# Convolution taps as diagonal matmuls, sums copied out by the scalar engine, gate product on GpSimd, front steps reordered

## The reference

```python
h   = concat(patch_embed(x), text_embed(...))       # (64, 48, 192)
x1  = layernorm(h)
# bidirectional Mamba, inner width 384, 16 states, 4 taps; dir 1 runs over the reversed sequence
xz  = x1 @ in_w.T;  xc, z = split(xz)
xconv = conv_b + sum(conv_w[:, k] * xpad[:, k:k + L, :] for k in range(K))   # K = 4
u   = silu(xconv)
dtx, Bm, Cm = split(u @ xproj_w.T)
dt  = softplus(dtx @ dt_w.T + dt_b)
h_t = exp(dt * A) * h_{t-1} + dt * Bm * u            # 16 states a channel
y   = sum_n(h_t * Cm) + u * D
y   = y * silu(z)                                    # the gate
out = y @ out_w.T
# layernorm, residual, then a mixture of 8 experts (top 2), expert width 768
```

## Time and profile before

| | us |
|---|---|
| three runs, median (lowest, highest) | 2037.2 (2034.75, 2037.57) |
| the profiled execution, its own time | 2037.6 |
| its span, first to last instruction | 2035.9 |
| TensorE matmul busy | 1523.3 (75%) |
| VectorE busy | 1514.1 (74%) |
| GpSimd busy | 1056.5 (52%) |
| ScalarE busy | 861.1 (42%) |

### The profile page before, as it was taken

How to read it: one execution, slowest core, us unless ns; L and a number is a source line. 1 busy time by engine, 2 the same in 40 slices (tenths; PEclk the granted TensorE clock), 3 DMA queues, 4 the chain that set the end, 5 groups by cost and what they waited for, 6 DMA issues and landing times. The chain is left out here.

```text
span 2035.9 us, 19521 instructions
## 1 busy us (share of the span) xinstructions
PE 1523.3 (75%) x4714; PEld 866.1 (43%) x4715; DVE 1514.1 (74%) x1780; ACT 861.1 (42%) x1848; POOL 1056.5 (52%) x539
## 2 busy tenths in 40 slices
PE   6566776776677677767767775876643899999997
PEld 4233343343344334434433443443332566666665
DVE  3699999999999999999999999999954122222221
ACT  2555545554554555455455454554510222222221
POOL 2465676675667657655675675548600233333332
PEclk8777897888788778878878887888875999999999
DMA  3412303031231303122130402213025411111111
GB/s 80 148 48 79 119 29 136 21 129 52 85 114 35 136 16 133 38 99 97 53 120 18 147 37 100 85 42 136 0 73 133 114 26 24 25 24 24 26 24 22
DMA packets 49182, 144.71 MB, mean 71 GB/s; under 512 B 13118, under 2 KB 26028, under 8 KB 48332
## 3 DMA queue, kind: packets, MB, share of 16 engines
q1 hardware_dynamic: 36956, 129.61, 18.7%
q0 software_dynamic: 12144, 14.30, 4.2%
HBM read 132.67 MB, written 11.21 MB: 71 GB/s over the span
## 5 line engine op out<-in xcount | busy, mean ns | idle before, releaser
L629 POOL TENSOR_TENSOR ring<-dtu,brep 128x1536 f32<-128x1536 f32 x192 | 661.0, 3447 | 446.0 <-DVE states L640 316.3
L652 PE MATMUL py<-ring,ident 128*128 128x384 f32 x1536 | 637.2, 568 | 133.7 <-DVE yg L669 110.5
L640 DVE TENSOR_TENSOR_SCAN states<-states,ring 128x768 f32<-128x768 f32 x384 | 673.7, 1755 | 30.2 <-ACT states L616 14.7
L652 PEld LDWEIGHTS py<-ring,ident 128*128 128x128 f32 x1536 | 332.7, 223 | 420.6 <-issue 186.2
L616 ACT ACTIVATE states<-dt_,aneg 128x376 f32<-128x376 f32 x768 | 406.1, 560 | 0.0
L642 DVE TENSOR_TENSOR ring<-states,crep 128x768 f32<-128x768 f32 x384 | 367.6, 957 | 13.2
L613 ACT ACTIVATE states<-zero_cols 128x16 f32<-128x16 f32 x384 | 71.2, 186 | 642.7 <-DVE ring L642 637.6
L1288 PE MATMUL gu<-w,xsT 96*128 x660 | 298.3, 602 | 7.2 <-issue 6.6
L462 PE MATMUL pf<-xT,wxz 97*128 97x384 f32 (+1 forms) x384 | 183.7, 624 | 139.0 <-ACT xT L449 55.3
L1329 DVE COPY yidx<-place 128x1 int32 (+1 forms) x56 | 8.4, 153 | 250.8 <-DMA out_tokens<-ys,yidx 250.8
L1288 PEld LDWEIGHTS gu<-w,xsT 96*128 96x128 f32 x660 | 122.6, 193 | 145.6 <-issue 145.6
(11 more groups left out here) (221 smaller groups left out, 1412.3 us busy)
## 6 DMA issues: line engine op xcount, KB each, us to landing
brep<-b_c_rows SPq DMA_DIRECT2D x64, 768.0 KB, 4.1
crep<-b_c_rows SPq DMA_DIRECT2D x64, 768.0 KB, 4.6
w<-in_w SPq DMA_DIRECT2D x8, 1152.0 KB, 14.2
wd<-in_wd SPq DMA_DIRECT2D x8, 576.0 KB, 16.3
ptok<-in_p_tok SPq DMA_DIRECT2D x8, 384.0 KB, 3.8
pT<-in_p_T SPq DMA_DIRECT2D x8, 384.0 KB, 4.8
out_tokens<-h SPq DMA_DIRECT2D x8, 288.0 KB, 2.1
x_scratch<-x SPq DMA_DIRECT2D x8, 288.0 KB, 2.9
```

The costliest lines, as they stand in the source:

```text
L629: gp.tensor_tensor(ring[:, w % NRING], dtu[:, d, o, :].unsqueeze(1).to_broadcast([128, GN, T]), brep[:, ng], ALU.mult).then_inc(dbu_ok, 1)
L640: v.tensor_tensor_scan(h_in, h_in, x_in, 0.0, ALU.mult, ALU.add).then_inc(scan_ok, 1)
L652: mm = pe.matmul(py[:, 0:T], ident[:], ring[:, w % NRING, i, :], start=(ng == 0 and i == 0), stop=False)
```

## The change

Four edits, one after the other:

1. The convolution leaves VectorE. At setup VectorE builds 12 diagonal matrices (3 tiles x 4 taps) from the identity. `pe_conv` adds all four taps of a tile in PSUM with them; the moving operand is a shifted window of `xc`. ScalarE no longer writes the scaled copy. The bias is added when a tile is read: tile 0 by a copy to `ea` in its own step, tiles 1 and 2 in the SiLU itself. The SiLU is three instructions of one tile instead of one of three, and it comes ahead of the SiLU of z, which has its own semaphore.
2. The sums leave `py` by ScalarE (`act_y`), unit `TAKEN` = 4 after the tile's start, at the end of a unit's main work; the next tile's first sum waits for this copy (`y_sb`).
3. The gate product is done by GpSimd in place in `yg` (`pool_gate`), one unit later, behind that unit's ring fill.
4. One table `DIR` replaces `DIR0` and `DIR1`. A front matmul stands one unit after the copy that it waits for or that frees its bank; the step times are made as tiles 0 and 1, then 2, instead of 0, then 1 and 2. Most steps of `BACK` are one unit later; `xT_out` is one earlier.

```diff
+        tap_diag = sb("tap_diag", [128, NC, KC + 1, 128])
...
+            conv = [(f"cv{d}_{o}", 1) for o in range(NC)]
             rest = [(f"bc{d}", 1)] + [(f"dt{d}_{o}", 1) for o in range(NC)]
-            FJOBS += x + rest + z if d == 0 else x + z[:2] + rest + z[2:]
+            FJOBS += x + conv + rest + z
...
-            if tiles[0] == 0:
-                wait(act, dv.sem, dv.after("dt", e - 1))
...
-                    act.activation(out, p[:, 0:T].rearrange("p (b l) -> p b l", b=CB), ACT.Copy)
-
-                    op = act.activation(ea[:, o, :], p[:, 0:T], ACT.Identity, scale=cw[:, o, KC:KC + 1], bias=cb[:, o:o + 1])
+                    op = act.activation(out, p[:, 0:T].rearrange("p (b l) -> p b l", b=CB), ACT.Copy)
...
+        def pe_conv(pe, c, d, tiles):
+
+            for o in tiles:
+                job_read(pe, f"xz{d}_{o}", c)
+                p = job_start(pe, f"cv{d}_{o}", c)
+                for k in range(KC + 1):
+                    at = k if d == 0 else 2 * KC - k
+                    mm = pe.matmul(p[:, 0:T], tap_diag[:, o, k, :], xc[:, o, :, at:at + L], start=(k == 0), stop=(k == KC))
+                mm.then_inc(jsem(f"cv{d}_{o}", "full"), 1)
+
+        def act_conv(act, c, d):
 
             e = 2 * c + d
...
+            p = job_wait(act, f"cv{d}_0", c)
+            wait(act, dv.sem, dv.after("dt", e - 1))
+            act.activation(ea[:, 0, :], p[:, 0:T], ACT.Identity, bias=cb[:, 0:1]).then_inc(jsem(f"cv{d}_0", "free"), 1)
 
         def act_silu(act, c, d):
 
             e = 2 * c + d
             act.preload_act_table_set("silu_and_others")
+            if not isinstance(c, int) or c < NCH:
+                job_read(act, f"cv{d}_0", c)
+                wait(act, y_ok, UD * (e - 1))
+                act.activation(u[:, d, 0], ea[:, 0], ACT.Silu).then_inc(ds.sem, 1)
+                for o in range(1, NC):
+                    p = job_wait(act, f"cv{d}_{o}", c)
+                    act.activation(u[:, d, o], p[:, 0:T], ACT.Silu, bias=cb[:, o:o + 1]).then_inc(jsem(f"cv{d}_{o}", "free"), 1)
             if not isinstance(e, int) or e > 0:
...
-                op = act.activation(zs[:, 1 - d], zs[:, 1 - d], ACT.Silu)
...
-                op = act.activation(u[:, d], ea[:], ACT.Silu)
-            op.then_inc(ds.sem, 1)
+                act.activation(zs[:, 1 - d], zs[:, 1 - d], ACT.Silu).then_inc(zs_ok, 1)
             act.preload_act_table_set("natural_log_exp_and_others")
...
             if ng == 0:
-                wait(pe, gated, NC * e + o)
+                wait(pe, y_sb, NC * e + o)
...
+        def act_y(act, c, d, o):
+
+            wait(act, qfull, QJ * (c - 1) + 2)
+            act.wait_ge(filled, 32)
+            act.wait_ge(y_ok, U2 * c + UD * d + NG * (o + 1))
+            for lo, hi in ((0, LI), (LI, L)):
+                yv = py[:, 0:T].rearrange("p (b l) -> p b l", b=CB)[:, :, lo:hi]
+                op = act.activation(yg[:, d, o, CB * lo:CB * hi].rearrange("p (b l) -> p b l", b=CB), yv, ACT.Copy)
+            op.then_inc(y_sb, 1)
+
+        def pool_gate(gp, c, d, o):
 
             e = 2 * c + d
...
+            gp.wait_ge(zs_ok, e + 1)
+            gp.wait_ge(y_sb, NC * e + o + 1)
             for lo, hi in ((0, LI), (LI, L)):
...
+                op = gp.tensor_tensor(yv, yv, zv, ALU.mult)
             op.then_inc(gated, 1)
...
+                for k in range(KC + 1):
+                    v.tensor_scalar(tap_diag[:, o, k, :], ident[:], cw[:, o, k:k + 1], None, ALU.mult)
...
-                 7: ["embed", "embed_rs"], 8: ["x1"], 9: ["xT"], 10: ["xT_out"]}
-        DIR0 = {-2: ["x01"], -1: ["x01_out", "x2"], 0: ["x2_out", "conv01"], 1: ["conv2", "silu", "bc"],
-                2: ["bc_out"], 3: ["bc_store"], 4: ["dt0"], 5: ["dt12", "dt0_out"], 7: ["dt12_out", "softplus"],
-                8: ["z01"], 9: ["steps", "z01_out", "z2"], 10: ["z2_out"]}
-        DIR1 = {-2: ["x01"], -1: ["x01_out", "x2"], 0: ["x2_out", "conv01"],
-                1: ["z01", "conv2", "silu", "z01_out"], 2: ["bc", "bc_out"], 3: ["bc_store"], 5: ["dt0"],
-                7: ["dt0_out", "dt12"], 8: ["dt12_out", "softplus", "z2"], 9: ["z2_out", "steps"]}
-        BACK = {2: ["out01"], 3: ["out01_add", "out2"], 4: ["out2_add"], 5: ["rs"], 6: ["h2"],
-                8: ["stat3", "rs3"], 9: ["x3"], 15: ["x3T0"], 17: ["x3T0_out", "x3T1"], 19: ["x3T1_out"],
-                20: ["router"], 23: ["logits"]}
+                 7: ["embed", "embed_rs"], 8: ["x1"], 9: ["xT", "xT_out"]}
+        DIR = {-2: ["x01"], -1: ["x01_out"], 0: ["x2", "conv0", "x2_out", "conv0_out"], 1: ["conv12", "silu"],
+               3: ["bc", "bc_out"], 4: ["bc_store", "dt01", "dt01_out"], 5: ["dt2"], 6: ["dt2_out", "softplus"],
+               7: ["z01", "z01_out"], 8: ["steps", "z2", "z2_out"]}
+        BACK = {3: ["out01"], 4: ["out01_add", "out2"], 5: ["out2_add"], 6: ["rs"], 7: ["h2"],
+                9: ["stat3", "rs3"], 10: ["x3"], 16: ["x3T0"], 18: ["x3T0_out", "x3T1"], 20: ["x3T1_out"],
+                21: ["router"], 23: ["logits"]}
...
-        GATE = NG + 1
+        TAKEN = NG
...
+            for step, at in (("y_out", TAKEN), ("gate", TAKEN + 1)):
...
-                yield from gates[w]
                 yield "scan", c, w
...
+                yield from taken[w]
                 yield from slots[w]
```

More of the change, by code:

```diff
@@ L505, in act_silu @@
                 job_read(act, f"xz{before[1]}_{2 * NC - 2}", before[0])
-                op = act.activation(zs[:, 1 - d], zs[:, 1 - d], ACT.Silu)
-            if not isinstance(c, int) or c < NCH:
-                act.wait_ge(dv.sem, dv.after("conv2b", e))
-                wait(act, y_ok, UD * (e - 1))
-                op = act.activation(u[:, d], ea[:], ACT.Silu)
-            op.then_inc(ds.sem, 1)
+                act.activation(zs[:, 1 - d], zs[:, 1 - d], ACT.Silu).then_inc(zs_ok, 1)
             act.preload_act_table_set("natural_log_exp_and_others")
@@ L516, in pe_bc @@
             pe.wait_ge(ds.sem, ds.after("silu", e))
+            for o in range(1, NC):
+                job_read(pe, f"cv{d}_{o}", c)
             p = job_start(pe, f"bc{d}", c)
@@ L656, in pe_sum @@
             mm.then_inc(y_ok, 1)
[L658 removed]
+        def act_y(act, c, d, o):
[7 more added lines that the diff above has]
+        def pool_gate(gp, c, d, o):
             e = 2 * c + d
[L662 to L665 removed]
+            gp.wait_ge(zs_ok, e + 1)
+            gp.wait_ge(y_sb, NC * e + o + 1)
             for lo, hi in ((0, LI), (LI, L)):
[L667 to L669 removed]
+                zv = zs[:, d, o, :].rearrange("p (b l) -> p b l", b=CB)[:, :, lo:hi]
+                yv = yg[:, d, o, CB * lo:CB * hi].rearrange("p (b l) -> p b l", b=CB)
+                op = gp.tensor_tensor(yv, yv, zv, ALU.mult)
             op.then_inc(gated, 1)
@@ L943, in plan @@
                             spread[w + U2].append(("spread", c + 1, (d, ng, which)))
-            gates = [[] for _ in range(U2)]
-            for d in range(2):
-                for o in range(NC):
-                    w = UD * d + NG * o + GATE
-                    if w < U2:
-                        gates[w].append(("gate", c, (d, o)))
-                    elif not first:
-                        gates[w - U2].append(("gate", c - 1, (d, o)))
-            put(DIR1, 0, c, 1)
+            taken = [[] for _ in range(U2)]
+            for step, at in (("y_out", TAKEN), ("gate", TAKEN + 1)):
+                for d in range(2):
+                    for o in range(NC):
+                        w = UD * d + NG * o + at
+                        if w < U2:
+                            taken[w].append((step, c, (d, o)))
+                        elif not first:
+                            taken[w - U2].append((step, c - 1, (d, o)))
+            put(DIR, 0, c, 1)
             if not first:
@@ L994, in prologue @@
             gates = ("z01", "z01_out", "z2", "z2_out")
-            direction = list(in_order(DIR0, 0, 0))
+            direction = list(in_order(DIR, 0, 0))
             yield from [step for step in direction if step[0] not in gates]
@@ L1004, in prologue @@
             yield from [step for step in direction if step[0] in gates]
-            yield from in_order({w: DIR1[w] for w in DIR1 if w < 0}, 0, 1)
+            yield from in_order({w: DIR[w] for w in DIR if w < 0}, 0, 1)
         def epilogue():
@@ L1069, in _ @@
                 "ahead": pool_input,
+                "gate": lambda e, c, k: pool_gate(e, c, *k),
                 "h2": lambda e, c, k: None if at_end(c) else norm_h2(e, c),
@@ L1105, in _ @@
                 "x1": lambda e, c, k: dve_x1(e, c),
-                "conv01": lambda e, c, d: dve_conv(e, c, d, (0, 1)),
-                "conv2": lambda e, c, d: dve_conv(e, c, d, (2,)),
                 "steps": dve_steps,
-                "scan": dve_scan, "gate": lambda e, c, k: dve_gate(e, c, *k),
+                "scan": dve_scan,
                 "out01_add": lambda e, c, k: dve_out(e, c, (0, 1)),
```

42 lines of the change are left out of this document (14 added, 28 removed).

## The result

The changed kernel takes 1963.1 us (median of 4 runs, 1959.6 to 1964.7) against 2037.4 for the kernel before; the ratio is 0.9632, 95% interval 0.9618 to 0.9646. That is 74 us less. The forecast was 1938 us in a range of 1893 to 1988: the direction and the mechanism held, and a quarter of the forecast gain did not come.

A forecast was written before the change was run, and what follows sets the result against it. VectorE was taken to set the end of every chunk. From 2037.6 us, -144 - 12 + 40 + 7 + 3 + 4.5 + 1 gave 1937, stated as 1938, range 1893 to 1988.

The forecast's parts named there:

- What leaves VectorE: In the chunks, convolution (112 us) and gate product with its waits (32 us) leave VectorE, all on the path: 144 us.
- The SiLU stall in direction 0: Next chunk's direction 0: VectorE stalls 3.6 us, 2.4 from ScalarE's excess work and 1.2 waiting for taps; 7 times, 25 us.
- In direction 1: SiLU stall where patch statistics in unit 1 move VectorE's next scan by 1.7 us: 1.9 us, 8 times, 15 us.
- Units 4 and 6 of the next chunk's direction 0: ScalarE's copies and step times run 0.6 and 0.4 us over: 1.0 us, seven times, 7 us.
- The gate on GpSimd: Each gate takes GpSimd 1.2 us (bounds 0.6 and 2.0), with nothing on the path but meetings with VectorE's work.
- rivals 2 and 3: TensorE reaches the taps at half clock, in about half the directions (1990 us, chance 0.11) or all (2070 us, 0.04).
- rival 4: At the chunk's start GpSimd falls behind, one ring fill late by 4.6 us a chunk: 37 us, 1975 us; chance 0.07.
- What goes of stalls: The sine step, now alone in its unit, stops delaying a scan: 12 of the 14.7 us of VectorE's decay waits go.
- 3 us in all for VectorE's work that meets a gate: VectorE work with two SBUF inputs held up by GpSimd's new gates: 3 us in all, bounds 0 and 58.
- Moves that I cost at nothing: B/C store, results, norms and routing go one unit later, and front matmuls leave their copies' unit: 0 us.
- The prologue: Before the chunks: 12 more diagonals (3.4 us) and an exposed convolution on TensorE, 2 to 10 us later; 4.5 us taken.

The follow-up runs named there:

- e3: Changed kernel with the SiLU of u and z replaced by same-size copies and the two table loads around them left out; 1953.1 us.
- e5: Changed kernel with TensorE doing the taps of tiles 1 and 2 before the sum of unit 0 in unit 1; 1956.6 us.
- e2: Changed kernel with the sums' copy and GpSimd's gate undone: VectorE multiplies the sums out of PSUM with the gate; 1969.6 us.
- e6: Changed kernel with most of the gate product left out: GpSimd multiplies one column of each sequence and piece instead of all 48; 1961.9 us.
- e4: Changed kernel with VectorE's range reduction in unit 4 instead of unit 3; 1929.6 us.
- e7: Changed kernel with three edits together: sums copied into their own buffer, range reduction in unit 4, taps before the sum; 1919.7 us.
- e1: Changed kernel with ScalarE copying the sums into their own buffer, so GpSimd's gate, not the copy, waits for the output matmuls; 1942.8 us.
- e10: Kernel before the change with the range reduction in unit 4 instead of unit 3, and nothing else; 2021.7 us.
- e8: Changed kernel with front matmuls no longer set one unit behind the copies (xT_out, x2 and B/C projection moved back); 2001.8 us.

## Why the prediction was right, and where it was off

Right: VectorE set the end of every chunk, and its gain is bounded by what ScalarE can hide. Point by point:

- What leaves VectorE, 144 us: between the first and the last scan the convolution had 112.7 us with its wait, the gates 33.4 with theirs. The scans behind them, which overlapped with them a little, are now 3.8 us longer in sum, so 142 us left.
- The SiLU stall in direction 0, 3.6 us: measured 3.43 to 3.46. e3 and e5 confirm its two parts, ScalarE's own excess (2.3 left in e5; 2.4 forecast, though the terms 1.28 + 3 x 0.5 + 1.07 + 1.28 make 5.13 and not 5.2) and the wait for the taps (1.08 us in the chunk shown; 1.2 forecast). This was the term on which the forecast rested.
- In direction 1, 1.9 us: 1.67 to 2.0 in the first three chunks, 3.3 in the four that follow a turn of the loop, 3.45 in the last, which has no patch statistics. Behind a turn the trace shows a 2.5 us gap on VectorE, then TensorE idle for 3.77 us and its next sum taking 4.54 instead of 2.75 us, which is partly half clock. That is about 7 us more. It was read from the trace and not tried by itself; e2, where the sum does not wait for ScalarE's copy, has 0.46 us there.
- Units 4 and 6 of the next chunk's direction 0, 1.0 us a chunk: 0.3 to 0.6.
- The gate on GpSimd, 1.2 us and off the path: 1.14, and e6 shows no cost clear of the spread.
- Half clock as the decider (rivals 2 and 3): no. The taps run at the full clock in every direction, sixteen records in 5.4 us. The granted clock of a chunk rose from 0.83 to 0.92, with TensorE idle for 37 of 169 us where it had been idle for 51 of 178.
- GpSimd late at the chunk's start (rival 4): not in this kernel, where the only wait for the ring is the prologue's 4.7 us, as before. It is what e4 and e7 uncover.

Off, and this is the missing 25 us:

- "What goes of stalls ... I take 12 of the 14.7 us off" failed. The sine step's wait did not go, it grew to 2.0 to 2.8 us and got a second one of 1.07 behind it, 21.6 us in all. I worked ScalarE's 4.4 us of sine work against its unit, and overlooked the wait on `qfull` at the head of the new copy one unit earlier, although it stands in the diff: with the output matmuls one unit later and the copy one unit ahead of the old gate, both fell into unit 4.

The first fence is TensorE, the second ScalarE, in unit 4 of the changed kernel:

```profile
794.85 4.05 PE L692 MATMUL pq<-w2t,yg 128*128 128x192 f32 x12 [6.70 <-DVE h L703]
```

```profile
799.46 0.55 ACT L670 ACTIVATE yg<-py 128x128 f32<-128x128 f32 x2 [3.91 <-PE pq L693]
```

The output matmuls wait 6.70 us for VectorE's addition, end at 799.4, and only then does the copy start, 3.91 us late, with the step times behind it. e1 takes this wait away: 20 us.

- "3 us in all for VectorE's work that meets a gate" was mis-sized and looked at the wrong pair. The step that met GpSimd was the range reduction, and it met ring fills. The three lines grew from 37.8 to 61.8 us, while the first image instruction, which took 18.9 us in all before, took 3.4, and the step times' first product grew by 2.9, by one meeting in the last chunk (4.29 us instead of 1.35): 24.0 - 15.5 + 2.9 = 11 us. e6 clears the gate; e10 and e4 show the size of the hold-up, 13.5 us in the kernel before and 33.1 in the changed one, where VectorE comes sooner. The rule from the Trainium skill (SBUF — State Buffer, "Who interferes with whom") stood, since in every run the scans kept 1754 to 1756 ns and, against the kernel before, of VectorE's work in the chunks only instructions with both inputs in SBUF grew by more than 4%. I applied it to the new GpSimd work alone, and not to the old work that VectorE would now reach sooner.
- "Moves that I cost at nothing": within the changed kernel the new order is worth 39 us (e8). The forecast of the stalls had it inside, since it counted TensorE's times in that order, but the text called it free.
- The prologue was 1.2 us longer (the first step times begin at 71.16 instead of 69.99), 4.5 forecast.

The waits for decays, 76.5 us, are 24.1 behind the SiLU step in direction 0 (forecast 25), 22.3 in direction 1 (15), 2.8 in units 4 and 6 (7), 21.6 behind the sine step and the unit after it (2.7), and 5.7 in the prologue's directions and the last chunk.

The sum can be done over between the first and the last scan of the eight chunks, in the kernel before (first line) and the changed one (second):

```profile
79.63:1486.34 1406.71, 1005.27 (x2714) 543.51 (x2712) 1342.85 (x1342) 725.33 (x1621) 897.89 (x401) 0.84 0.22 78
```

```profile
80.80:1409.39 1328.59, 1039.87 (x3074) 577.04 (x3072) 1217.74 (x1113) 733.10 (x1715) 927.47 (x495) 0.90 0.23 82
```

That is 78.1 us less. What left (-142.2), the waits for decays (+ 61.6), the three groups held up by GpSimd (+ 11.4), VectorE's waits for the output matmuls, which are gone (- 4.1), and the other step-time instructions and gaps under 0.1 us (- 4.4) make -77.7. The prologue (+ 1.2), the epilogue and routing up to its last scan (+ 1.2) and the rest of the program, which the change does not touch (+ 2.7), give the 73.1 us between the two profiled spans. That rest takes 512.0 to 515.4 us in the profiled executions of the kernels here, so its 2.7 us say nothing about the change.

## What to carry to other kernels

Work taken off the bounding engine had also been the cover for steps of other engines: list each such step with what it needs and what the unit leaves it, and do it for every wait at the head of a new instruction, not only for the instruction's length. An engine that gets faster comes sooner to the instructions of the engine that holds it up, so its old instructions must be set against the neighbour's old ones again, in the new order of time. When a second and third edit give less than alone, look at the engine that was not touched: here three edits left VectorE waiting for GpSimd's queue, and moving four gathers by four units gave 22 us.

## What had not been expected of the hardware

The hold-up goes both ways, and the two engines take turns. GpSimd's two fills beside the range reduction of the chunk shown above, together and the second alone:

```profile
778.99 7.55 POOL L634 TENSOR_TENSOR ring<-dtu,brep 128x1536 f32<-128x1536 f32 x2 [0.18 <-POOL dtu L629]
```

```profile
782.39 4.15 POOL L634 TENSOR_TENSOR ring<-dtu,brep 128x1536 f32<-128x1536 f32 x1
```

The product that VectorE begins at 780.23 ends at 783.25, which is 0.8 us after the first fill's end (782.43). The next, begun at 783.28, ends at 787.35, again 0.8 us after the end of the second fill (786.54). Alone such a product takes 0.96 us, so the two were held for 2.1 and 3.1. The second fill, begun while the first product was still open, takes 4.15 us instead of 3.44, so that the two fills take 7.55 us where two take 6.9 elsewhere. In another chunk (437.46 and 441.57) two products of 0.96 us take 4.07 us each, one behind the other.
